# A macaron layer on one core: decay constants computed before the first half step, and products of weights into a spare PSUM bank ahead of chosen waits

## The reference

```python
x = x + 0.5 * ffn(layernorm(x))      # "A": 256 -> 768 -> 256, weights int32 times 1/127
x = x + ssm(layernorm(x))            # "B"
x = x + 0.5 * ffn(layernorm(x))      # "C": the same weights as A

ffn(x): silu(x @ wg.T) * (x @ wu.T) @ wd.T
ssm(x): x_in, z = split(x @ in_proj.T)             # 512 channels each
        xc      = causal convolution of x_in, 4 taps, per channel, + bias
        dt, Bm  = parts of xc @ x_proj.T           # 16 and 128 columns
        delta   = clip(softplus(dt @ dt_proj.T + dt_b), 0.001, 0.1)
        A       = -exp(A_log);  A_bar = exp(delta * A);  B_bar = (A_bar - 1) / A * Bm
        h_t     = A_bar_t * h_(t-1) + B_bar_t      # scan over 2048 tokens, 128 states
        out     = (h @ C_proj.T + xc * D) * silu(z) @ out_proj.T
```

## Time and profile before

| | |
|---|---|
| runs | 544.32, 540.81, 538.62 us; median 540.81 |
| the profiled execution's own time | 548.71 us |
| its span, first to last instruction | 546.8 us |
| mean granted TensorE clock | 0.968 |
| busy: TensorE, VectorE, ScalarE, GpSimd | 507.3, 416.7, 281.1, 227.0 us |

### The profile page before, as it was taken

How to read it: one execution, slowest core, us unless ns; L and a number is a source line. 1 busy time by engine, 2 the same in 40 slices (tenths; PEclk the granted TensorE clock), 3 DMA queues, 4 the chain that set the end, 5 groups by cost and what they waited for, 6 DMA issues and landing times.

```text
span 546.8 us, 7716 instructions
## 1 busy us (share of the span) xinstructions
PE 507.3 (93%) x2657; PEld 296.1 (54%) x2657; DVE 416.7 (76%) x865; ACT 281.1 (51%) x472; POOL 227.0 (42%) x192
## 2 busy tenths in 40 slices
PE   4869877999999999999999999999999999998696
PEld 4346423844566465745485456646484557545444
DVE  5786678699678977798769977897869876887332
ACT  5473655076624774187606672377508761674032
POOL 2230053428271637246451828154633736073213
PEclk9887997999999999999999999999999999999869
DMA  8401000000220020101120032003020021000001
GB/s 290 119 0 41 2 0 0 2 2 0 41 80 1 2 41 32 47 1 22 30 69 0 2 41 78 1 2 40 20 59 2 10 33 40 1 1 20 19 2 40
DMA packets 27240, 16.84 MB, mean 31 GB/s; under 512 B 15264, under 2 KB 26528, under 8 KB 27184
## 3 DMA queue, kind: packets, MB, share of 16 engines
q1 hardware_dynamic: 26368, 15.26, 11.1%
q10 hardware_dynamic: 816, 0.79, 0.5%
HBM read 8.71 MB, written 4.19 MB: 24 GB/s over the span
## 4 chain that ended last, share of the span: by engine, by line
PE 73%; DVE 12%; DMA 5%; ACT 3%; issue 3%; SPq 2%; POOL 2%; POOLq 0%; DVEq 0%; ACTq 0%
PE q L1346 49%; PE dp L1346 19%; DMA xt<-xs 4%; DVE xn L773 3%; PE tp L1257 3%; SPq L379 2%; DVE xs L790 2%; DVE h L803 1%; DMA hh<-in_L_ffn_w_gate_dram 1%; POOL xcl L428 1%; PE q L1257 1%; ACT xc L566 0%; DVE rmx L947 0%; DVE ser L860 0%; DVE x L814 0%
## 5 line engine op out<-in xcount | busy, mean ns | idle before, releaser
L421 POOL TENSOR_TENSOR hl<-h,hh 128x512 f16<-128x512 f32 x96 | 121.1, 1274 | 107.2 <-ACT hh L558 106.9
L803 DVE SCALAR_TENSOR_TENSOR h<-sg,hsm,q 128x512 f32<-128x512 f32 x96 | 70.7, 742 | 39.3 <-PE q L1346 26.2
L828 DVE SCALAR_TENSOR_TENSOR xc<-xi,cw,xc 128x512 f32<-128x512 f32 x96 | 84.1, 890 | 3.2 <-ACT xi L574 2.6
L532 ACT ACTIVATE xh<-tp 128x512 f16<-128x512 f32 x36 | 19.5, 595 | 113.8 <-PE tp L1257 113.8
L550 ACT ACTIVATE sg<-q 128x512 f32<-128x512 f32 x96 | 56.6, 591 | 40.8 <-PE q L1346 40.8
L558 ACT ACTIVATE hh<-h 128x512 f16<-128x512 f32 x96 | 60.3, 629 | 27.4 <-DVE h L803 27.1
L428 POOL TENSOR_TENSOR xcl<-xc,xch 128x512 f16<-128x512 f32 x32 | 41.1, 1296 | 50.4 <-ACT xch L581 50.4
L1346 PE MATMUL dp<-wo,yu 128*128 128x256 f32 x256 | 60.2, 388 | 1.5 <-POOL yu L436 1.5
L1346 PE MATMUL dp<-wd,hh 128*128 128x256 bf16 x384 | 53.9, 277 | 0.9 <-ACT hh L558 0.9
L1346 PE MATMUL dp<-wd,hl 128*128 128x256 bf16 x384 | 53.7, 277 | 0.8 <-POOL hl L421 0.8
L1346 PEld LDWEIGHTS dp<-wo,yu 128*128 128x128 f32 x256 | 48.4, 195 | 9.5 <-POOL yu L436 2.7
(11 more groups left out here) (182 smaller groups left out, 851.0 us busy)
## 6 DMA issues: line engine op xcount, KB each, us to landing
xpre<-in_L_attn_x_dram SPq DMA_DIRECT2D x8, 512.0 KB, 4.5
out_dram<-x SPq DMA_DIRECT2D x16, 256.0 KB, 2.1
xc<-in_L_attn_in_proj_w_dram SPq DMA_DIRECT2D x1, 1024.0 KB, 11.1
hl<-in_L_ffn_w_up_dram ACTq DMA_DIRECT2D x3, 256.0 KB, 6.5
hh<-in_L_ffn_w_gate_dram SPq DMA_DIRECT2D x3, 256.0 KB, 7.1
hh<-in_L_ffn_w_down_dram SPq DMA_DIRECT2D x1, 768.0 KB, 8.5
yu<-n_L_attn_out_proj_w_dram SPq DMA_DIRECT2D x1, 512.0 KB, 4.0
yu<-in_L_attn_x_proj_w_dram SPq DMA_DIRECT2D x1, 256.0 KB, 11.4
```

Source lines behind the costliest of these rows:

```text
L421: pool.tensor_tensor(HL[g.f][:, c, :], H[:, j, :], HH[g.f][:, c, :], ALU.subtract)\
L532: act.activation(XH[g.f][:, kc, :], tp[kc][:, :], ACT.Copy, scale=XS).then_inc(t_hi[kc], 1)
L803: dve.scalar_tensor_tensor(out=H[:, first % 3, :], in0=SG[:, first % 2, :], scalar=HSM[:, c:c + 1], in1=q[bank][:, :], op0=ALU.mult, op1=A ...
L828: dve.scalar_tensor_tensor(out=XC[s][:, m, :], in0=XI[s][:, m, k:k + TILE], scalar=CW[:, m, k:k + 1], in1=XC[s][:, m, :], op0=ALU.mult, op ...
```

## The change

It has two parts. On VectorE `decay_rate` and `decay_series` (12 instructions) are issued at the end of the start, behind `x_proj_unscale`, and `decay_finish` (8 instructions) just ahead of `delta_in` in half step 0.

On TensorE a new function `keep_busy` issues matmuls whose result nobody reads: weights times weights (bfloat16, 512 columns) or, where the weights aren't there yet, the identity with itself (`early`, float32, 128 columns), into a bank of tp. They carry no semaphore. They stand ahead of: the first turned weights (16 early), the first turned XN (8 early), the turned maxima (8), each of the eight waits of `xp0` in half step 0 (2 each), up3 of block A in half step 0 (10), the C projection of half step 7 (9), the four waits of its out projection (1 each), the turned XN of half step 8 (18), and the twelve waits of its down projection (1 each).

```diff
--- before.py
+++ after.py
@@ -1137,6 +1137,8 @@
             hidden(second, "A", (0, 1))
             norm_lo(first, "Bnext")
             x_proj_unscale()
+            decay_rate()
+            decay_series()
 
             def half(g):
                 B, C, A = g.has("B"), g.has("C"), g.has("A")
@@ -1198,14 +1200,12 @@
                     normalize(g, "A", (2, 3))
                     split_lo(g, (0,))
                 if B:
+                    if g.h == 0:
+                        decay_finish()
                     delta_in(g)
                 if A and g.h > 0:
                     split_lo(g, (1,))
                 if B:
-                    if g.h == 0:
-                        decay_rate()
-                        decay_series()
-                        decay_finish()
                     delta(g)
                     series(g, (0, 1, 2, 3))
                 if A and g.h > 0:
@@ -1258,6 +1258,14 @@
 
             readers = {"sg": sg_ready, "h": h_ready, "bm": bm_ready, "pc": pc_ready, "ix": xi_ready,
                        "iz": sz_ready, "cp": yu_half, "w_act": w_act, "w_dve": w_dve}
+
+            def keep_busy(n, bank, early=False):
+
+                for _ in range(n):
+                    if early:
+                        pe.matmul(bank[:, 0:P], IDN[:, :], IDN[:, :], start=True, stop=True)
+                    else:
+                        pe.matmul(bank[:, :], WG[:, 0, 0:P], WG[:, 0, 0:TILE], start=True, stop=True)
 
             def turn_weights(bank, w, j):
 
@@ -1321,6 +1329,10 @@
                 if part == 0:
                     for kc in range(KD):
                         wait(pe, t_lo[kc], g.number("turn", k))
+                    if k == "A" and g.h == -1:
+                        keep_busy(8, tp[0], early=True)
+                    elif k == "C" and g.h == LAST:
+                        keep_busy(18, tp[0])
                 pe.wait_ge(xn_ready, 2 * g.number("norm", k) + part + 1)
                 for b in (2 * part, 2 * part + 1):
                     for kc in range(KD):
@@ -1334,10 +1346,11 @@
                 n = g.number("turn", k, 1, back)
                 return {kc: (t_hi[kc], n) for kc in range(KD)} | {low + kc: (t_lo[kc], n) for kc in range(KD)}
 
-            def accumulate(out, terms, more=(), over=None, waits={}):
+            def accumulate(out, terms, more=(), over=None, waits={}, busy=0):
 
                 for at, (w, a) in enumerate(terms):
                     if at in waits:
+                        keep_busy(busy, tp[0])
                         pe.wait_ge(*waits[at])
                     if more and at == len(terms) - 1:
                         with pe.If(over > 0):
@@ -1346,13 +1359,15 @@
                     ins = pe.matmul(out, w, a, start=(at == 0), stop=(at == len(terms) - 1))
                 return ins
 
-            def product(g, what, part, terms, more=(), waits={}):
+            def product(g, what, part, terms, more=(), waits={}, busy=0):
 
                 who, count = g.before(what, part)
                 if who:
+                    if who == "bm" and g.h == 0:
+                        keep_busy(10, tp[0])
                     pe.wait_ge(readers[who], count)
                 bank = g.bank(what, part)[0]
-                accumulate(q[bank][:, :], terms, more, flag, waits).then_inc(q_full[bank], 1)
+                accumulate(q[bank][:, :], terms, more, flag, waits, busy).then_inc(q_full[bank], 1)
 
             def gate_up(g, k, what):
                 up, c = what[0] == "u", int(what[-1])
@@ -1383,10 +1398,12 @@
                          for m in range(IC) for low in range(2)}
                 product(g, f"xp{n}", "B", [(w[1 - n][:, m, :], part[:, m, :]) for m in range(IC)
                                            for w, part in ((WXH, XCH), (WXL, XCH), (WXH, XCL))],
-                        waits={} if n else ready)
+                        waits={} if n else ready, busy=2 if g.h == 0 else 0)
 
             def c_proj(g, m):
                 if m == 0:
+                    if g.h == LAST - 1:
+                        keep_busy(9, tp[0])
                     pe.wait_ge(hs_ready, g.index(1))
                 product(g, f"cp{m}", "B", [(WC[:, P * m:P * (m + 1)], HS[g.b][:, :])])
 
@@ -1398,7 +1415,8 @@
                     tok = slice(P * (2 * j + b), P * (2 * j + b + 1))
                     ins = accumulate(dp[j][:, D * b:D * (b + 1)], *([(a[:, c, tok], w[:, c, :]) for a, c, w in some]
                                                                     for some in (terms, more)),
-                                     over=flag_down, waits=waits if j == b == 0 else {})
+                                     over=flag_down, waits=waits if j == b == 0 else {},
+                                     busy=1 if g.h == LAST or k == "B" and g.h == LAST - 1 else 0)
                 if blocks[-1] == 1:
                     ins.then_inc(d_full[j], 1)
 
@@ -1441,12 +1459,15 @@
             products = steps.index(("gate0", "A", -1))
             rows = steps.index(("fill", "in", -1))
             delta_rows, tokens = steps.index(("fill", "delta", -1)), steps.index(("down00", "A", -1))
+            keep_busy(16, tp[0], early=True)
             run(steps[:products], first)
             count_over(0)
             flag = flag_value(0)
             further_parts(flag, [p for p in PARTS if p[0] != "d"])
             run(steps[products:rows], first)
 
+            pe.wait_ge(t_lo[1], 2)
+            keep_busy(8, tp[1])
             pe.wait_ge(xm_ready, 1)
             pe.matmul(tp[1][:, 0:P], XMB, IDN[:, :], start=True, stop=True).then_inc(xm_full, 1)
             run(steps[rows:delta_rows], first)
```

## The result

| | before | with the change |
|---|---|---|
| median of 20 runs each | 544.45 us (538.48 to 548.79) | 540.45 us (537.66 to 541.56) |
| the profiled execution, its span | 548.71, 546.8 us | 541.04, 539.1 us |
| mean granted clock of that execution | 0.968 | 0.997 |

The ratio is 0.9931, 95% interval 0.991 to 0.9951: the change takes off 0.7%, half of the 1.4% that was forecast, and 540.45 lies outside the predicted range. The profiled execution of before, at 548.71, was within 0.1 us of the slowest of the 20.

A forecast was written before the change was run, and what follows sets the result against it. TensorE's own work was taken to bound 91.6 to 508 us, VectorE the start. Terms summed to -9.55 us, or -5.4 without two falls; the middle, -7.5, gave 533.3 us, with 529.5 to 540.0 for 8 in 10.

The forecast's parts named there:

- I carry it on whole: After half step 0's C projection: its 4.1 us gain moves all later work forward, the steady half steps changing by 0.
- Half step 0: Column moved, fillings in xp0 and ten before up3: C projection starts 4.1 us earlier, bounded by the scan.
- the moved column costs nothing: The 20 column instructions fit VectorE's idle times ahead of L842; about 0.05 us left over, taken as nothing.
- The rival of the clock that yields nothing: Clock falls despite fillings or matters only in the trace; 540.8 us, or 539 with some of it; chance 0.15.
- The start: Up to the in projection: early fillings cost 0.45 us, the eight before the maxima give 2.4.
- if the clock then doesn't fall at 37: Condition behind the eight before the maxima: small product takes 1.0 us, not 2.04; second residual starts 2.4 us earlier.
- The nine: Before half step 7's C projection: 1.94 us of fillings in a 0.98 us wait, so products start 0.96 late.
- The four singles: One filling at each wait of half step 7's out projection: full clock makes the matmuls behind 1.75 us shorter.
- The twelve: One filling at each wait of the last down projection: costs 0.5 us, bounds +0.2 and +0.9.
- The eighteen: Before the last turned rows: 3.9 us of fillings in a 4.49 us wait keep the clock, gaining 3.2 us.
- The middle between two sums: Median gain taken as -7.5 us, between -9.55 with all clock falls and -5.4 without those at 37 and 508.
- the rival of few falls: The runs had few clock falls, so -5.4 us applies whole or less: 535.4 to 537 us; chance 0.23.

The follow-up runs named there:

- 318 in front: The whole change plus 156 instructions of one-column products in two idle places of TensorE's start: 538.10 us, ratio 0.9884 to before.
- before again: The kernel before, repeated with no edit: 544.15 us, ratio 0.999; its profiled execution took 544.10 us.
- 96 added: Decay column moved and the 18 fillings, against before, with 24 one-column products (96 instructions) added at the very start: 536.31 us, ratio 0.9846.
- 128 added: Decay column moved and the 18 fillings, against before, with 32 one-column products (128 instructions) added at the very start: 535.64 us, ratio 0.9858.
- the first four experiments: Kernel before unedited, decay column moved alone, fillings alone, whole change repeated: 544.15, 538.69, 541.85 and 539.91 us.

## Why the prediction was wrong

**"I carry it on whole" failed: +1.6 us.** This is one of the signs that I had named for being wrong, that the stretch of the steady half steps grows. I took the stretch from 91.6 to 508 as TensorE's own work, on which the edits ahead have no effect but to move it forward. Its trace had six waits of 2.4 us in total for xt, which I left out as unchanged. They hang on where the fetches of TensorE's code fall, and 162 more instructions move these: 358.6 becomes 360.2 and 359.6 in the two traces of the change (3.4 and 3.2 us of waits for xt, and 0.95 and 0.45 for the late output transfer). With 318 in front it is at 355.8, so this one term is worth up to 4.4 us.

**"Half step 0" held as a sum (-4.1; -4.3 and -4.8 measured) and failed as a story.** L847 behind the logarithm: held, within 0.04. That the moved column costs nothing: held in most traces. With it the convolution starts 4.50 us behind the in projection, before again 4.48, and L842 17.80 and 17.73; but L842 starts at 18.42 in both traces of the change, 0.3 later than with the fillings alone, and at 18.41 with 96 added: the last of the eight, L984, took 1.18 us there and 0.16 in the trace of the moved column. No run shows why. But the clock's part of the gain was put down to the ten fillings. The moved column alone shortens the wait to 1.42 us, the clock does not fall, and the stretch is 5.3 us shorter; the fillings then take back 0.97. I had worked out that the ten outlast the wait by 0.7, and did not ask what the clock would do in that short wait without them. The scan, my bound for the C projection, ended 4.4 us earlier relative to the in projection and not 2.5, mostly because it and the copy before it took 1.45 us and not 3.1. The rival of the clock that yields nothing counts the column at 2.5 too, and is wrong for the same reason.

**The start (+0.45 - 2.4 = -1.95): nothing against the ordinary before.** The step that failed is "if the clock then doesn't fall at 37": it fell at 42.3. The eight do shorten the wait for the maxima to 0.4 us, but then the product at 39.89 waits 1.69 for VectorE, where it waited 0.87, and behind this wait the clock is at 0.50 from 42.3 to 45.7. All five traces with the start fillings have such a fall between 40.6 and 47.6. What it costs shows beside the one trace, with 128 added and no start filling, whose granted clock is 1.00 from 41.4 to 46.8; the start of `down` and of what follows it, with the change, then there:

```profile
41.54 0.83 PE L1359 MATMUL dp<-wd,hh 128*128 128x256 bf16 x6 [0.56 <-issue]
...
48.46 1.91 PE L1257 MATMUL q<-idn,yu 128*128 128x128 f32 x16
```

```profile
41.47 0.83 PE L1357 MATMUL dp<-wd,hh 128*128 128x256 bf16 x6 [0.56 <-issue]
...
46.72 1.91 PE L1257 MATMUL q<-idn,yu 128*128 128x128 f32 x16
```

6.92 us and 5.25. I had computed 41.5, 5.3 and 46.8, so the price of the full clock was right, and in that trace the in projection starts at 55.36, 1.7 earlier than with the change. The forecast lost it because the time won ahead of VectorE's product turned into a new wait. The first turned weights start 0.7 earlier than in the earlier trace rows, which is scatter: over the eleven traces without start fillings they start between 7.31 and 7.87, over the five with them between 7.14 and 8.43.

**The nine (+0.96): +0.81. The four singles (-1.75)**: right in size (7.54 to 5.88), but only 3 of the ten traces without them lose it. **The twelve (+0.5): +0.50.**

**The eighteen (-3.2): -1.35** (39.58 to 38.23). I took 522.0 to 528.5 at the lower level from the one profiled execution. In the ordinary one it ends at 522.7, though the wait ahead of it is as long. From the residual to `down` pass 17.7 us with the 18 alone, against 20.3 in the profiled before and 19.1 in the ordinary one: 2.6 and 1.4. So the mechanism was right, and 1.2 of the size came from the longest case. The other 0.6 is in the turned blocks, which from their start to the next product gave 0.5 and not 0.9 (they took 1.30 us and not 1.04), and in the work behind them, 2.1 and not 2.3. I had asked which falls are optional, and named two, but took this one's full length as certain.

**The middle between two sums** failed as well: an ordinary execution of before is the rival of few falls. Its -5.4, with the start at 0 for +0.45, the end 1.6 dearer and the fetches' 1.6, gives about -2.7, where the traces have -3.1 and the medians -4.0. The base of 540.81 was off too, to my advantage: from 544.45 my -7.5 gives 537.0, 3.5 below what came. The runs of before show the falls directly: over the 23 timed beside the first four experiments the mean granted clock lies between 0.971 and 0.984 and the time between 540.6 and 548.8, 4.0 us less for each 0.01, with a correlation of -0.78. The three later sets, of 16, 7 and 10 runs, give 3.4, 5.8 and 2.3 us, so the sign is firm and the size is not. The change narrows its runs to 3.9 us, from 10.3.

## What to carry to other kernels

Take a dependence off the chain first and look at what the clock does then; here the fillings in a wait that had become short cost their overrun and returned nothing, and those ahead of a product that another engine bounds moved the fall to the next wait. Profile the kernel before twice before you price a clock fall, since one execution can hold falls that most do not have. And when a stretch that you did not edit changes its length, look where the fetches of the longest instruction list lie against its DMA transposes: 64 idle instructions at the start moved this kernel's steady stretch by 2.2 us, where the whole change gave 4.0 by the medians.

## What the runs showed of the hardware

The fetches of code are 40 packets and 0.66 MB for the kernel before, some 16 KB each, and their places come back after 256 more instructions on TensorE's list. (That list is longer than its records: it holds products behind branches that aren't taken.) A fetch within 3.2 us of the start of a pair of transposes put off the second one's landing from 4.40 to 4.74 us to 4.87 to 5.86, and in 55 of 57 cases TensorE by 0.16 to 1.06 us; fetches from 3.7 us on did not. Whether the fetch takes the DMA engines' time or holds the transpose's own path was not tried.

64 records of products of one column took 1.74 us in all: cheap instructions for moving code.

Matmuls of the identity with itself ran from 1.52 us with nothing ahead of them: 32 records in 5.36 us, and the next 16 in 1.95. At the 0.23 us that I had for such a product at the full clock 16 of them would be 3.7 us, so a part of the first block ran at a slower pace, as the first turned weights did before. The traces have no record of the granted clock before 13.1 us (before) and 4.7 us (the change), so the level there is read from the pace alone.
